# A selective scan with attention beside it: a pass covers two directions of one image instead of one direction of two images

## The reference, cut to what matters

```python
# layer 0 (on the group-normed image): a selective scan in K = 4 directions
xz = x @ in_proj_w.T; xh, z = split(xz)                     # 96 channels each
xc = silu(depthwise_conv3x3(xh) + conv_b)
x_hwwh = stack([flat(xc), flat(transpose(xc))])              # rows, columns
xs = concatenate([x_hwwh, flip(x_hwwh, -1)])                 # and both backwards
dts, Bs, Cs = split(einsum(xs, x_proj_w))                    # 12, 16, 16 rows
dts = softplus(einsum(dts, dt_projs_w) + dt_projs_b)
h = h * exp(dt * A) + (dt * u) * B;  y = sum_n(h * C)        # 256 steps, 96 x 16 states
y = sum of the 4 directions, turned back, + D * xs
x = x + (layernorm(y) * silu(z)) @ out_proj_w.T
# layer 1: Performer attention, 12 heads of 16, 64 ReLU features
out = qp @ (kp.T @ v) / (qp @ sum(kp));  x = x + out @ w_proj.T + b_proj
# layer 2: softmax attention in 6 of the 12 heads, which a router picks by the image
logits = mean(hidden) @ Wr; top 6; softmax(q k.T / 4) @ v per picked head; layernorm
```

## Time and profile before

| | |
|---|---|
| median of 3 runs | 508.72 us (507.52 to 510.63) |
| profiled execution: its own time | 506.69 us |
| its span, first to last instruction | 504.8 us |
| mean granted TensorE clock | 0.839 of full |
| first `scan` starts | 50.5 us |
| last `scan` (unit 95) ends | 326.2 us |
| busy: PE, DVE, ACT, POOL | 399.8, 379.4, 182.3, 199.1 us |

### The profile page before, as it was taken

How to read it: one execution, slowest core, us unless ns; L and a number is a source line. 1 busy time by engine, 2 the same in 40 slices (tenths; PEclk the granted TensorE clock), 3 DMA queues, 4 the chain that set the end, 5 groups by cost and what they waited for, 6 DMA issues and landing times. The chain is left out here.

```text
span 504.8 us, 5418 instructions
## 1 busy us (share of the span) xinstructions
PE 399.8 (79%) x1545; PEld 221.4 (44%) x1545; DVE 379.4 (75%) x732; ACT 182.3 (36%) x442; POOL 199.1 (39%) x199
## 2 busy tenths in 40 slices
PE   5511485878796856959999988999999999889882
PEld 4300121224232312415466465456665849676541
DVE  6354799998999999999789899885376364353574
ACT  2253443346463633522433323233324220334340
POOL 4414585658586866754454644510010010000011
PEclk9555787769897988857999999965999996958987
DMA  6403120110112111111010100000000000000000
GB/s 132 76 5 72 44 59 12 45 31 13 45 38 53 31 40 35 26 33 32 16 42 23 26 0 1 0 2 0 2 16 2 0 0 17 1 0 1 1 16 16
DMA packets 15742, 12.66 MB, mean 25 GB/s; under 512 B 7280, under 2 KB 11362, under 8 KB 15714
## 3 DMA queue, kind: packets, MB, share of 16 engines
q1 hardware_dynamic: 15713, 12.33, 10.6%
HBM read 2.62 MB, written 0.79 MB: 7 GB/s over the span
## 5 line engine op out<-in xcount | busy, mean ns | idle before, releaser
L528 POOL TENSOR_TENSOR outp<-state,c_rep 128x512 f32<-128x512 f32 x96 | 128.8, 1346 | 93.7 <-PE y_acc L1323 50.0
L948 DVE TENSOR_TENSOR_SCAN state<-decay,inp_bc 128x512 f32<-128x512 f32 x96 | 117.2, 1221 | 6.7 <-DVE inp_bc L939 3.2
L1323 PE MATMUL y_acc<-outp,band 128*96 128x512 f32 x192 | 114.1, 681 | 7.2 <-DVE y_sum L963 3.2
L690 ACT ACTIVATE decay<-step_bc,a_neg 128x510 f32<-128x510 f32 x96 | 64.9, 683 | 57.8 <-PE step_bc L1310 57.6
L939 DVE TENSOR_TENSOR inp_bc<-b_rep,inp_bc 128x512 f32<-128x512 f32 x96 | 65.4, 681 | 9.9 <-PE inp_bc L1314 9.8
L472 POOL TENSOR_TENSOR rs<-mv,neg_half 128x2 f32<-128x2 f32 x16 | 11.3, 706 | 152.0 <-DVE mv L984 149.8
L1314 PE MATMUL inp_bc<-stack,spread 96*128 96x512 bf16 x96 | 42.1, 439 | 36.6 <-DVE state L948 36.3
L1310 PE MATMUL step_bc<-stack,spread 96*128 96x512 bf16 x96 | 40.9, 426 | 16.9 <-DMA stack<-lo 14.3
L1323 PEld LDWEIGHTS y_acc<-outp,band 128*96 128x96 f32 x192 | 35.1, 187 | 24.3 <-issue 10.4
L1314 PEld LDWEIGHTS inp_bc<-stack,spread 96*128 96x128 bf16 x96 | 9.9, 103 | 78.2 <-DVE state L948 72.3
L1310 PEld LDWEIGHTS step_bc<-stack,spread 96*128 96x128 bf16 x96 | 10.5, 110 | 38.4 <-issue 30.3
(11 more groups left out here) (376 smaller groups left out, 709.4 us busy)
## 6 DMA issues: line engine op xcount, KB each, us to landing
b_rep<-bc SPq DMA_DIRECT2D x64, 32.0 KB, 2.0
c_rep<-bc SPq DMA_DIRECT2D x64, 32.0 KB, 2.0
stack<-hi SPq DMA_DIRECT2D x24, 64.0 KB, 2.0
stack<-mid SPq DMA_DIRECT2D x24, 64.0 KB, 2.0
stack<-lo SPq DMA_DIRECT2D x24, 64.0 KB, 2.0
x_tok<-in_x_dram SPq DMA_DIRECT2D x2, 384.0 KB, 3.8
out_dram<-room_g SPq DMA_DIRECT2D x4, 192.0 KB, 2.0
room_a<-in_L_attn_w_qkv_dram SPq DMA_DIRECT2D x1, 432.0 KB, 6.5
```

The lines of the kernel that those rows point to most:

```text
L528: g.tensor_tensor(outp[:, u % SLOTS, :], state[:, u % STATE_SLOTS, :], c_rep[:, n % 2, :], ALU.mult).then_inc(S["outp"], 1)
L690: a.activation(decay[:, u % SLOTS, :, 1:L], step_bc[u % 2][:, :].rearrange("p (b l) -> p b l", b=IMG)[:, :, 1:L], ACT.Exp, scale=a_neg[:, ...
L948: v.tensor_tensor_scan(state[:, u % STATE_SLOTS, :], decay[:, u % SLOTS, :, :].rearrange("p b l -> p (b l)"), inp_bc[u % 2][:, :], 0.0, AL ...
L1323: t_.matmul(y_acc[0:DI, :], band[:, at:at + DI], outp[:, u % SLOTS, :], start=(g12 == 0), stop=(g12 == UNITS - 1)).then_inc(S["y_mm"], 1)
```

## The change

A pass now covers one image `m` in two directions (`PER_IMAGE = 2` passes an image; `d = 0` rows and columns, `d = 1` both backwards); the 512 columns are two directions of 256 pixels. Image 0 is through after pass 1, image 1 after pass 3, and so on, so that `side_work` can give an image its attention steps from unit 24(n + 1) + 4 on: 80 attention steps of images 0 to 2 stand beside the passes (45 before), and 68 are left in `rest` (103 before). With it:

- `conv`, `silu` and `z` are made image by image; only image 0's `xh`, `conv`, `silu` stand ahead of pass 0, and `z` of all images beside passes 1 and 2;
- the decays of a unit take two ScalarE instructions of 255 columns instead of one of 510, since the two directions have different `A`; the reading of the projection likewise takes two;
- `LAG` is gone: every engine takes a side step in the same unit;
- the preparing of a pass is moved two units later, for the `lo` parts from unit 6 to unit 8 of 12;
- weights' steps follow each other every unit from unit 5 on instead of every second from 14 on.

```diff
-LAG = 1
-PRE_RAW, PRE_CLIP, PRE_EXP, PRE_SERIES, PRE_LN = -4, -3, -2, -1, -1
-PRE_MAX, PRE_MAX_SERIES, PRE_INP = 0, 1, 2
-PRE_HI, PRE_REST, PRE_MID, PRE_LO = (2, 3), (4, 5), (5, 6), (6, 6)
+PRE_RAW, PRE_CLIP, PRE_EXP, PRE_SERIES, PRE_LN = -2, -1, 0, 1, 1
+PRE_MAX, PRE_MAX_SERIES, PRE_INP = 2, 3, 4
+PRE_HI, PRE_REST, PRE_MID, PRE_LO = (4, 5), (6, 7), (7, 8), (8, 8)
...
-SCANS = HALVES * DIRS
+PAIR = 2
+PER_IMAGE = DIRS // PAIR
+SCANS = IMAGES * PER_IMAGE
...
-FRONT_BESIDE = ((1, "xh"), (8, "conv0"), (16, "conv1"), (19, "silu"), (21, "z"))
-WEIGHTS_FIRST = 14
-UNITS_AFTER = {step: 1 for step in ("q0", "q1", "q2", "kv00", "kv01", "kv10", "wqk", "wv", "fq", "fk")}
-UNITS_AFTER_ELSE = 2
+FRONT_BESIDE = ((0, "xh", 1), (1, "conv0", 1), (2, "conv1", 1), (3, "sig", 1), (4, "silu", 1),
+                (6, "xh", 2), (8, "conv0", 2), (9, "conv1", 2), (10, "sig", 2), (11, "silu", 2),
+                (12, "xh", 3), (14, "conv0", 3), (15, "conv1", 3), (16, "sig", 3), (17, "silu", 3),
+                (18, "z", 0), (19, "zg", 0), (20, "z", 1), (21, "zg", 1), (22, "z", 2), (23, "zg", 2), (24, "z", 3), (25, "zg", 3))
+WEIGHTS_FIRST = 5
+UNITS_AFTER = {"o": 2, "p": 2, "yT": 2, "yn": 2, "lg": 2, "fo": 2}
+UNITS_AFTER_ELSE = 1
...
-    done, ready = [0, 0], [DIRS * UNITS + FIRST_STEP, DIRS * UNITS + FIRST_STEP + 1]
-    for u in range(DIRS * UNITS, SLOT_COUNT):
+    done = [0] * IMAGES
+    ready = [PER_IMAGE * UNITS * (n + 1) + FIRST_STEP for n in range(IMAGES)]
+    for u in range(PER_IMAGE * UNITS, SLOT_COUNT):
...
+            if not may_follow(step, done[n - IMG] if n >= IMG else None, steps):
+                continue
...
-                at = u % (DIRS * UNITS)
-                a.activation(decay[:, u % SLOTS, :, 1:L],
-                             step_bc[u % 2][:, :].rearrange("p (b l) -> p b l", b=IMG)[:, :, 1:L],
-                             ACT.Exp, scale=a_neg[:, at:at + 1]).then_inc(S["decay"], 1)
+                for e in range(PAIR):
+                    at = (PAIR * (u // UNITS % PER_IMAGE) + e) * UNITS + u % UNITS
+                    a.activation(decay[:, u % SLOTS, e, 1:L], step_bc[u % 2][:, e * L + 1:(e + 1) * L],
+                                 ACT.Exp, scale=a_neg[:, at:at + 1]).then_inc(S["decay"], 1)
...
-                        window = xpad[:].rearrange("p b y x -> p (b y) x")[:, i // 3:i // 3 + ACC_ROWS, i % 3:i % 3 + SIDE]
+                        window = xpad[:, m % IMG, i // 3:i // 3 + SIDE, i % 3:i % 3 + SIDE]
...
                 dve.wait_ge(S["drive"], u + 1)
-                dve.wait_ge(S["decay"], u + 1)
+                dve.wait_ge(S["decay"], PAIR * (u + 1))
...
-                for item in beside[u - LAG] if u >= LAG else []:
+                for item in beside[u]:
                     side(*item)
```

More of the change, by code:

```diff
@@ L91, in side_work, with may_follow @@
+WEIGHTS_FIRST = 5
+UNITS_AFTER = {"o": 2, "p": 2, "yT": 2, "yn": 2, "lg": 2, "fo": 2}
+UNITS_AFTER_ELSE = 1
+NO_PRODUCT = {"yn", "tn", "un", "rn", "conv0", "conv1", "sig", "silu", "zg"}
+def may_follow(step, done, steps):
+    if done is None:
+        return True
+    after = {"tT": "fv", "un": "fo"}.get(step)
+    return after is None or done > steps.index(after)
 def side_work():
     beside = [[] for _ in range(SLOT_COUNT)]
-    for at, step in FRONT_BESIDE:
-        beside[at].append((step, 1))
+    for at, step, n in FRONT_BESIDE:
+        beside[at].append((step, n))
@@ L114, in side_work @@
             ready[n] = u + UNITS_AFTER.get(step, UNITS_AFTER_ELSE)
-    at = {step: i for i, step in enumerate(steps)}
-    done += [0, 0]
     rest = []
@@ L558, in _ @@
                         left_of_mid(preparing(u, PRE_LO[i]), i)
-                for item in beside[u - LAG] if u >= LAG else []:
+                for item in beside[u]:
                     side(*item)
             weigh(SLOT_COUNT - 1)
-            for item in beside[SLOT_COUNT - LAG]:
-                side(*item)
             for item in rest:
@@ L631, in _ @@
             front("xh", 0)
-            front("silu", 0)
-            group_normed(1)
+            for m in range(1, IMAGES):
+                group_normed(m)
+            front("sig", 0)
             def weights(step):
@@ L720, in side @@
                     weights(step)
-                elif step in ("xh", "z", "silu"):
+                elif step in ("xh", "z", "sig"):
                     front(step, n)
@@ new lines, in front @@
+                    if m == IMAGES - 1:
+                        for h in range(IMG):
+                            v.memset(wsel[h][:], 0.0).then_inc(S["wsel_zero"], 1)
+                if step == "zg":
+                    h, ts = m // IMG, slice(2 * (m % IMG), 2 * (m % IMG) + 2)
+                    dve.wait_ge(S["z_kept"], m + 1)
+                    dve.wait_ge(S["gate_e"], 2 * (m + 1))
+                    v.tensor_tensor(z[:, h, ts, :], z[:, h, ts, :], ze[:], ALU.mult).then_inc(S["gate_s"], 1)
@@ L1084, in side @@
                     weights(step)
-                elif step in ("conv0", "conv1", "z", "silu"):
+                elif step in ("conv0", "conv1", "zg", "silu"):
                     front(step, n)
```

265 lines of the change are left out of this document (124 added, 141 removed).

## The result

The changed kernel takes 572.55 us (median of 4 runs, 571.89 to 573.76) against 509.68 for the kernel before on the same chip: a ratio of 1.1252, interval [1.1202, 1.1303]. The ratio leaves out one slow run of the kernel before (518.53, where its other three took 507.52 to 510.63). The profiled span grew from 504.8 to 570.1, by 65.3 where the prediction had 18. The sign was right; the size was far outside the range.

The account below looks back on a forecast made before the run. The prediction took VectorE to bound the passes and TensorE, with its waits, the tail. Its terms, -7 + 40 + 6 - 2 + 14 + 12 + 5 - 50 = +18, added to the median of 508.72 gave 527 us, range 502 to 545.

Parts of the forecast that it names:

- startup: Ahead of pass 0, only one image is convolved, with smaller operations: -7 us (-8 to -4).
- VectorE busy in the passes: Beside the passes: moved attention work +40 us, smaller convolutions +6, first unit -2, GpSimd contention +12.
- wait before the scan for ScalarE: In 12 head units, the exponential stands ahead of the next decay, so VectorE idles 1.3 us each: +14 (0 to 18).
- other idle time of VectorE in the passes (TensorE): Beside the passes, runs of TensorE-limited steps and side steps waiting for TensorE in their own unit: +5 us (0 to 12).
- tail: Behind the last scan, 68 steps instead of 103 take 128.2 us against 178.8: -50 (-61 to -44).
- the idle time in the heads' units: Sign: in units of h0 to h5, ScalarE's decay ends VectorE's idle time before the scan, over 10 us in all.
- passes 5 and 7: Sign: these two passes take above 50 us.
- The contention with GpSimd: Beside the passes, GpSimd's product slows VectorE's divisions and norm scalings: +12 us (0 to 14).
- "Faster": Rival: tail -61, ScalarE wait and contention absent, TensorE +0; -24, so 485 us; chance 0.14.
- "no change": Rival: only one of the two mechanisms, ScalarE wait or GpSimd contention, with tail -61; -5, so 504 us; chance 0.13.
- The late stack: Rival: in the passes, `lo` transfers come 2.7 us late where units 8 to 11 are light; +19, 546 us; chance 0.05.
- The rival of the clock: Rival: TensorE spends more units of the passes at 1.2 GHz; with the tail's rest +16, 543 us; chance 0.12.

Follow-up runs that it names:

- Experiment 5: The kernel of Experiment 1 with GpSimd's product with C cut to 64 of the 512 columns, leaving work out; 515.99 us, ratio 1.0152.
- experiment 6: The kernel before the change with GpSimd's product with C cut to 64 of 512 columns; 507.18 us (three runs, no interval), against 508.17.
- Experiment 1: The changed kernel with ScalarE issuing the decays of the next unit ahead of the side step instead of behind it; 541.64 us, ratio 1.0658.
- experiment 2: The changed kernel with the lag put back: GpSimd, ScalarE and VectorE take a side step one unit after TensorE; 574.23 us, ratio 1.1321.
- experiment 4: The changed kernel with the decays first and no step from h0 on beside the passes; 533.36 us, no interval.
- experiment 7: The kernel of Experiment 1 with the two softmax divisions of a step on ScalarE instead of VectorE; 541.03 us, ratio 1.0629.
- experiment 8: The kernel of Experiment 1 with one extra, overwritten bf16 matmul of 512 columns ahead of each product of the tail, 80 in all; 547.32 us, ratio 1.0776.
- experiment 10: The kernel before the change with each unit's decay in two ScalarE instructions of 255 columns instead of one of 510; 516.84 us, no interval, against 508.45.

## Why the prediction was wrong, step by step

The spans' difference of 65.3 beside the terms (VectorE's busy time and its idle time in the passes, cut as above, with what stood before):

| step | predicted | measured |
|---|---|---|
| startup | -7 | -5.5 |
| VectorE busy in the passes (moved work, convolutions, first unit, GpSimd) | +56 | +60.7 |
| wait before the scan for ScalarE | +14 | +35.1 |
| other idle time of VectorE in the passes (TensorE) | +5 | +10.7 |
| tail | -50 | -35.7 |
| sum | +18 | +65.3 |

(38.6 of idle time that the row puts down to something, "issue" included, stand before the scans, where it was 3.5; the rest of the idle time is 26.4 and was 15.7.) Of the miss of 47.3 the wait for ScalarE has 21, the tail 14, the other idle time 6, VectorE's busy time 5.

Of the signs named ahead, the first scan (45.0), the division (0.85), the idle time in the heads' units (12.7), passes 5 and 7 (60.4 and 53.3) and TensorE's share of the tail (83%) came as said; the last scan's end (427.2 for 394) and the tail (142.9 for 128) did not. The sign on passes 5 and 7 looked in too few places: passes 0 and 6 were above 50 as well (50.8 and 53.5), and pass 0, which has no attention step, grew by 14.4.

**Startup: right.** The first scan is at 45.0; `xh` of one image takes 2.0 against 3.70 and eight convolution operations 3.8 against 6.5.

**VectorE's busy time: right in sum,** within 5 of 61, in part by luck. The contention with GpSimd, put at 12 from two instances in the earlier trace rows and from the earlier trace rows, is in it, and experiments 5 and 6 give it about 20; what is left, 41, had been put at 44, so two errors offset each other. Part of the missing contention lies in the convolutions: with the operation that starts each, the 27 small ones took 18.8 beside the passes where the nine large ones took 9.4, against a forecast of 13.5 and 8. The price per division (847 against 390 ns) is +0.46; the earlier trace rows had given +0.375. The Trainium skill (GPSIMD Engine Reference, Specifications) says that GpSimd's SBUF interfaces are shared with VectorE, with contention against VectorE instructions in a two-port mode or with two SBUF inputs. The trace agrees that the two engines contend (711 to 484 ns for the convolution when GpSimd's product is cut); whether the division runs in a two-port mode no run here shows, and the size of the loss stands in these runs alone.

**The wait for ScalarE: the step that failed.** "1.3 of VectorE's idle time in each of 12 steps (h0 to h5 of images 0 and 1)" was right for those twelve: 6.5 and 6.2 us in their two stretches, 1.27 in a plain unit. What was wrong is that it stopped there: 14 were forecast, and 35.1 more than before were measured. The order that puts a side step ahead of the next decay holds for every unit, and I asked for it only where I had looked at it, at the heads. The other 28 of the 40.6 us are spread over the rest: 10.7 in passes 0 and 1, where unit 10's timeline shows the projection, a `sig` step and copies of weights ahead of the decays, and the others among units with `kv`, `cx`, `fq` and the like, whose copies stand there too. Experiment 1 settles it: with one call moved ahead these waits are gone, and 31 us with them.

**TensorE beside the passes: mis-sized,** 10.7 instead of 5, with the waits for the products of q, cr, the attention row and the heads. That `LAG` had a part in it experiment 2 does not bear out: with the lag back these waits stayed. Since experiments 1, 4 and 7 all traded part of their gain for this wait (4, 20 and 13 us), it is the bound that stands next behind VectorE.

**Tail: mis-sized by 14; the clock is the likely cause, not a shown one.** The forecast took 68 steps at the rate of the last 124.6 us before. There TensorE was busy 105.7 at a granted clock of 0.86 and idle 18.9; in the new tail it is busy 118.3 at 0.73 and idle 24.6. Busy time times clock is 90.9 and 86.4. So the work is 4.5 less and the idle time 5.7 more; the forecast had 5 less for lighter steps, 5 more for image 3 alone and 3.6 more for the last sums. What the forecast took as unchanged is the clock. At 0.84 to 0.86 the 86.4 would be 100 to 103 of busy time, and with the 24.6 of idle time 125 to 127, beside the forecast's 128.2; this is an estimate from modelled ends. Against it, experiment 8 raised the clock and the tail did not shorten. The Trainium skill (TensorE: Matmul & The Clock Gate, What's actually happening) says that activity releases the clock; experiment 8 agrees, 0.73 to 0.83 with 80 matmuls more. What it is in the new tail that lowers the clock stays open. From 484 to 513 us it stood at 0.59 with TensorE busy 27.6 of 29.0 by the records, and experiment 10 had 0.79 in a tail that was not changed.

**The rivals.** "Faster" (the mechanisms absent) and "no change" fall: both mechanisms are there. The late stack falls too: the spreading's idle time that ends with a `lo` transfer is 15.1 us now and was 14.3, and 14.4 of the 15.1 lie in the startup. The rival of the clock had a size near the tail's miss (16), but by luck: it put the cost in units of the passes, which went from 0.88 to 0.84 with TensorE not setting their length. One of its readings was wrong as well: in the earlier trace rows the clock's digit is 9 in the first slice, where TensorE's is 5 on the page, and 6 and 5 in slices 27 and 28, where TensorE is at 9. (VectorE's slices there stand at 7 to 9 from the fifth on, not at 9 throughout; nothing hangs on it.) The case that came, the ScalarE wait everywhere and the clock in the tail together, was in none of the rivals.

**Where the idea itself stands.** With the order mended the change still loses about 35 us (experiment 1). The work that leaves the tail frees TensorE where VectorE idled, and lands on VectorE beside GpSimd, where a division costs twice and a norm's scaling three times what it costs in the tail. Experiment 5, which takes most of that contention away by leaving work out, is still at 1.0152 of the kernel before, and at 515.99 against 507.18 for the kernel before with the same work left out: even then the move gives nothing back. (The lowest run of the sixth, 495.36, is 18 below the lowest of the fifth, 513.47.)

## What to carry to other kernels

When a side step is put into a unit, go through each engine's stream for what now stands ahead of the instruction that the critical engine waits for, in every kind of unit, not only in those that look dear; an engine that is busy 40% of the passes, as ScalarE here, can still be the wait. Make what the pacing engine needs next ahead of the side work, as experiment 1 did by moving one call. And price an operation by its neighbour: what takes 0.39 us in a stretch without GpSimd took 0.85 beside it.

## What the runs showed that was not expected

- An idle time put down to "issue" or to the engine's own previous instruction (25.2 and 10.7 us before the scans) was in fact a wait for ScalarE: moving ScalarE's decays removed it (0.2 left).
- A cut of GpSimd's product from 1.37 to 0.45 us saved VectorE 27.5 us of busy time for the same instructions, 8.6% of the passes' 319; in the old arrangement, where few operations stood behind the scan, 7.9.
- TensorE's clock in the same unchanged tail was 0.84, 0.81 and 0.79 in three profiled executions (the kernel before, experiments 6 and 10), and the tail 178.6, 187.2 and 188.5 long: differences under 10 us there are not an edit's. That the clock sets the length is not shown: over the whole span the kernel before took 504.8 at 0.839, 506.6 at 0.88 and 508.3 at 0.899 in three of its runs.
